# FFN stage of an early-fusion block: rows and gelu turned by transposing DMA transfers, with one step more between an image's parts

## What is computed

```python
def act_quant(x):
    scale = 127.0 / jnp.clip(jnp.max(jnp.abs(x), axis=-1, keepdims=True), 1e-05, None)
    return jnp.clip(jnp.round(x * scale), -128.0, 127.0) / scale
def bitlinear(x, w, g):
    xn = rmsnorm(x, g)            # x * rsqrt(mean(x*x) + 1e-6) * g
    return einsum('bsd,fd->bsf', act_quant(xn), weight_quant(w))
h = h + bitlinear(gelu(bitlinear(layernorm(h), w1, g1)), w2, g2)
```

## Time and profile before

| | us |
|---|---|
| median of 3 runs (lowest, highest) | 1649.14 (1647.32, 1652.2) |
| the profiled execution | 1650.61 |
| its span, first to last instruction | 1648.8 |
| busy over the span: PE, DVE, ACT, POOL | 1470.4, 1337.6, 1301.8, 1113.9 |
| granted TensorE clock, mean | 0.926 |
| FFN stage: from the first `v2` to the end of the span | about 436 |

### The profile page before, as it was taken

How to read it: one execution, slowest core, us unless ns; L and a number is a source line. 1 busy time by engine, 2 the same in 40 slices (tenths; PEclk the granted TensorE clock), 3 DMA queues, 4 the chain that set the end, 5 groups by cost and what they waited for, 6 DMA issues and landing times. The chain is left out here.

```text
span 1648.8 us, 54578 instructions
## 1 busy us (share of the span) xinstructions
PE 1470.4 (89%) x18602; PEld 1180.7 (72%) x18602; DVE 1337.6 (81%) x2848; ACT 1301.8 (79%) x2183; POOL 1113.9 (68%) x1495
## 2 busy tenths in 40 slices
PE   5799999999999999999999999999766777777775
PEld 2678888887887888888888888888655655555554
DVE  5488888888887887887888888887578999999996
ACT  1377877887877878878878878877578999999997
POOL 5456666666666666666666666666367888888886
PEclk8799999999999999999999999999767788878787
DMA  8434334343343343343343343342100000000001
GB/s 215 77 63 68 55 70 65 56 71 63 58 71 61 61 70 60 63 69 58 63 71 56 63 71 56 64 71 40 50 22 26 25 28 28 25 25 25 30 25 31
DMA packets 104195, 93.58 MB, mean 57 GB/s; under 512 B 22737, under 2 KB 94466, under 8 KB 104162
## 3 DMA queue, kind: packets, MB, share of 16 engines
q1 hardware_dynamic: 103394, 91.58, 29.4%
q0 software_dynamic: 768, 1.57, 0.4%
HBM read 74.12 MB, written 11.91 MB: 52 GB/s over the span
## 5 line engine op out<-in xcount | busy, mean ns | idle before, releaser
L1108 PE MATMUL ps<-w_eff,pix 124*112 124x193 f32 (+1 forms) x2048 | 408.4, 338 | 9.8 <-DMA pix<-side 7.3
L713 DVE TENSOR_REDUCE nmax<-ps 116x12 bf16<-116x1344 f32 (+2 forms) x192 | 302.9, 1577 | 117.2 <-PE ps L1203 117.1
L929 ACT ACTIVATE probs<-ps,isw 116x688 f32<-116x688 f32 x384 | 299.1, 832 | 80.5 <-PE ps L1230 79.7
L431 POOL TENSOR_TENSOR xsq<-xsq 124x784 f32<-124x784 f32 (+1 forms) x128 | 184.4, 1440 | 245.3 <-ACT xsq L922 240.3
L518 POOL TENSOR_TENSOR pix<-probs,g_b 112x192 f32<-112x192 f32 (+1 forms) x512 | 309.1, 634 | 40.8 <-ACT probs L1074 30.4
L1108 PEld LDWEIGHTS ps<-w_eff,pix 124*112 124x112 f32 (+1 forms) x2048 | 309.2, 167 | 36.6 <-issue 21.5
L461 POOL TENSOR_SCALAR_AFFINE_SELECT probs<-probs 116x464 f32<-116x464 f32 x384 | 227.8, 610 | 22.3 <-ACT probs L929 19.0
L911 ACT ACTIVATE pix<-xpix 54x896 f32<-54x896 f32 (+1 forms) x128 | 196.9, 1541 | 1.5
L1165 PE MATMUL ps<-xnT,wq_pad 97*128 97x228 f32 (+1 forms) x768 | 166.5, 366 | 0.0
L1334 PE MATMUL ps<-w1t,xpix 96*112 96x384 f16 (+1 forms) x512 | 132.2, 418 | 19.4 <-DVE xpix L809 17.9
L1165 PEld LDWEIGHTS ps<-xnT,wq_pad 97*128 97x128 f32 (+1 forms) x768 | 142.2, 192 | 3.1
(11 more groups left out here) (142 smaller groups left out, 3032.4 us busy)
## 6 DMA issues: line engine op xcount, KB each, us to landing
xpix<-in_x SPq DMA_DIRECT2D x192, 196.0 KB
rden<-den_rows SPq DMA_DIRECT2D x256, 85.5 KB, 2.1
out<-xpix SPq DMA_DIRECT2D x64, 87.0 KB
out<-xpix SPq DMA_DIRECT2D x64, 84.0 KB
xpix<-in_x SPq DMA_DIRECT2D x128, 34.1 KB
h_all<-shift_w SPq DMA_DIRECT2D x5, 768.0 KB, 13.1
pix<-side SPq DMA_DIRECT2D x64, 36.8 KB
pix<-side SPq DMA_DIRECT2D x64, 36.6 KB
```

The source lines that it names most:

```text
L431: nc.gpsimd.tensor_tensor(out_, a, b, ALU.add).then_inc(s_ssq, 1)
L713: V.tensor_reduce(dst, src, AX_X, ALU.max, negate=True).then_inc(s_mx, 1)
L929: A(probs[0:TB, g, 2 * e:2 * e + 2, :], ps[0:TB, 4 + 2 * e:6 + 2 * e, 0:SK], ACT.Exp, scale=isw[0:TB, 7:8]).then_inc(s_p, 1)
L1108: last = MM(ps_tok[tile][0:P, :], pix[0:HI, par, o, lo:lo + P], w_eff[0:HI, o, :], start=(o == 0), stop=(o == OFFS - 1))
```

## The change

- The transposes on PE and both copies out of PSUM (DVE L809, ACT L1067) are gone. SP starts a transposing DMA transfer for each instead, SBUF to SBUF: `q1T` from `q1` (128 rows of 512 float16, 4 blocks of 128 columns) and `q2T` from `q2` (128 rows of 1,536, 12 blocks). `q1`, `q1T`, `q2`, `q2T` have two buffers each. SP's step: store `y` of i-4, turn `q1` of i+1, turn `q2` of i-2.
- The 1536 stays in the turned values. In the first product, a row of `w1t` holds the weights' column sums and meets a column of -1536 in `q1`; the contraction is now split 128 and 65, not 96 and 96. In the second, a product of one row (K = 1) goes ahead of each tile's six. The column sums are made once, ahead of the stage (`weight_columns`: 10 products on PE, two copies on ACT). `w1_t` is laid out for this on the host.
- One step more between an image's parts: in step i, DVE makes `q2`'s scales for i-2 and `y` of i-4; ACT quantises i-2, then does the gelu and the squares of i; PE does the first product of i and the second of i-3; POOL does `v2` of i, then the roots of i (they were ahead of `v2`, those of i-1), with no wait for `f_r1`.
- DVE: `y` now stands behind the maximum of `v1`.
- Once: three memsets on DVE, two on POOL (rows 96 to 127 of `q2`), and the wait of PE's first product for the column sums. SP's turn of the first `q1` stands ahead of the transfers of the last image's attention.

```diff
...
-        q1 = part(xpix, 768, DIM).bitcast(F16).rearrange("p (t d) -> p t d", t=2)
-        q1T = part(xpix, 960, 2 * TB).bitcast(F16).rearrange("p (t c k) -> p t c k", t=2, c=2)
-        q2T = part(xpix, 1192, NCH * TB).bitcast(F16).rearrange("p (t c k) -> p t c k", t=2, c=NCH)
+        q1_all = part(xpix, 384, 512).bitcast(F16)
+        q1 = [part(xpix, 384 + 256 * b, 256).bitcast(F16) for b in range(2)]
+        q1T = [part(xpix, 896 + 256 * b, 256).bitcast(F16).rearrange("p (k r) -> p k r", r=128) for b in range(2)]
+        v1 = part(xpix, 2176, 4 * DIM).rearrange("p (b t d) -> p b t d", b=2, t=2)
+        q2 = [part(probs_f, 4 * WIDE, HIDDEN).bitcast(F16), part(w_eff_f, 0, HIDDEN).bitcast(F16)]
+        q2T = [part(src, at, HIDDEN).bitcast(F16).rearrange("p (k r) -> p k r", r=128)
+               for src, at in ((xpix, 1408), (w_eff_f, HIDDEN))]
+        ones_h = part(tok_f, 0, 64).bitcast(F16)
+        minus = part(tok_f, 64, 64).bitcast(F16)
+        w2_sum = part(tok_f, 128, DIM // 2).bitcast(F16)
...
+            def turn_first(m, p):
+                sp.wait_ge(f_q1, m + 1)
+                apart(sp)
+                sp.dma_start(q1T[p], q1[p], transpose=True).then_inc(f_t1[p], 16)
+
+            def turn_second(j, p):
+                sp.wait_ge(f_q2, j + 1)
+                apart(sp)
+                sp.dma_start(q2T[p], q2[p], transpose=True).then_inc(f_t2[p], 16)
+
+            def store(n):
+                sp.wait_ge(f_y, n + 1)
+                for tile, (lo, hi) in enumerate(((0, TA), (TA, TOK))):
+                    sp.dma_start(out[bass.ds(n, 1), lo:hi, :].rearrange("a t d -> (a t) d"),
+                                 y[0:hi - lo, tile, :]).then_inc(f_out, 16)
+
+            def ffn_step(i, b, new=True, mid=True, last_=True):
+                if last_:
+                    store(i - 4)
+                if new:
+                    turn_first(i + 1, 1 - b)
+                if mid:
+                    turn_second(i - 2, b)
+
             for n in range(IMAGES - 5, IMAGES):
+                if n == IMAGES - 1:
+                    ffn_step(-1, 1, mid=False, last_=False)
                 step_images(n, n % 2, place=n + 4 < IMAGES, load=False)
...
-            with sp.Fori(0, IMAGES) as n:
...
+            ffn_step(0, 0, mid=False, last_=False)
...
+            with sp.Fori(2, PAIRS - 1) as t:
+                for b in range(2):
+                    ffn_step(2 * t + b, b)
...
+            ffn_step(IMAGES + 3, 1, new=False, mid=False)
...
-            def ffn_step(i, b, mid=True):
-
-                if mid:
-                    pool.wait_ge(f_ssq, 2 * i)
-                    nc.gpsimd.tensor_tensor(roots[:, bass.ds(i * 4 + 6, 2)], gel_sum[:, 1 - b, :], expo[:, 0:2],
-                                            ALU.pow).then_inc(f_r1, 1)
...
-            ffn_step(0, 0, mid=False)
+            pool.wait_ge(s_front, IMAGES)
+            pool.wait_ge(s_o, GROUPS * IMAGES)
+            pool.wait_ge(s_rms, IMAGES - 1)
+            for k in range(2):
+                nc.gpsimd.memset(q2[k][96:128, :], 0.0).then_inc(f_rows, 1)
+                pool.wait_ge(f_rows, k + 1)
+
+            def ffn_step(i, b):
+
+                after(pool, f_q2, i - 1)
+                for tile, P in enumerate((TA, TB)):
+                    pool.wait_ge(f_g, 2 * i + tile + 1)
+                    if tile == 1:
+                        pool.wait_ge(f_v2, 2 * i + 1)
+                    for lo in range(0, HIDDEN, HIDDEN // 4):
+                        cols = slice(lo, lo + HIDDEN // 4)
+                        last = nc.gpsimd.tensor_tensor(v2[0:P, b, tile, cols], gel[0:P, b, tile, cols],
+                                                       g2_b[0:P, cols], ALU.mult)
+                    last.then_inc(f_v2, 1)
+                pool.wait_ge(f_v2, 2 * i + 2)
+                pool.wait_ge(f_ssq, 2 * i + 2)
+                nc.gpsimd.tensor_tensor(roots[:, bass.ds(i * 4 + 14, 2)], gel_sum[:, b, :], expo[:, 0:2],
+                                        ALU.pow).then_inc(f_r1, 1)
+
+            ffn_step(0, 0)
             ffn_step(1, 1)
             ffn_step(2, 0)
+            row_roots(IMAGES - 1)
             ffn_step(3, 1)
-            row_roots(IMAGES - 1)
-            with pool.Fori(2, PAIRS - 1) as t:
+            with pool.Fori(2, PAIRS) as t:
                 for b in range(2):
                     ffn_step(2 * t + b, b)
-            ffn_step(IMAGES - 2, 0)
-            ffn_step(IMAGES - 1, 1)
-            ffn_step(IMAGES, 0)
...
+            step(V.memset(ones_h, 1.0))
+            step(V.memset(minus, -MAGIC16))
+            step(V.memset(q1_all, -MAGIC16))
...
-            def copy_rows_turned(m):
...
             def weigh_steps(i, b):
-                after(dve, f_g, 2 * i)
+                after(dve, f_g, min(2 * i, 2 * IMAGES) if isinstance(i, int) else 2 * i)
                 V.tensor_tensor(ff_st[:, b, 40:44], ff_st[:, b, 28:32], w_step[:, :], ALU.mult).then_inc(f_step, 1)
 
-            def ffn_step(i, b, new=True, mid=True, last_=True, turned=True, steps_=True, between=None, skipped=0):
-
-                m, j, st = i + 1, i - 1, ff_st[:, b, :]
+            def ffn_step(i, b, new=True, mid=True, last_=True, steps_=True, between=None, skipped=0):
+
+                m, j, st = i + 1, i - 2, ff_st[:, b, :]
                 flinks[:] = [0, (i + 1) * F_LINKS - skipped]
                 if new:
-                    after(dve, f_q1, m - 1)
                     for tile, P in enumerate((TA, TB)):
                         ins = V.scalar_tensor_tensor(v1[0:P, b, tile, :], h_all[0:P, hcols(m, tile)],
                                                      mean2[0:P, bass.ds(m * 2 + tile, 1)], g1_b[0:P, :],
                                                      ALU.add, ALU.mult)
                     flinks[0] += 1
                     ins.then_inc(f_vc, 1)
+                if steps_:
+                    weigh_steps(i - 1, 1 - b)
+                if between is not None:
+                    between()
+                if new or mid:
+                    after(dve, f_q2, i - 3)
+                if new:
+                    dve.wait_ge(f_vc, flinks[1] + flinks[0])
+                    ins = V.tensor_reduce(st[0:TB, 24:26], v1[0:TB, b, :, :], AX_X, ALU.max,
+                                          apply_absolute_value=True)
                 if last_:
-                    o = i - 3
-                    dve.wait_ge(f_step, o + 3)
+                    o = i - 4
+                    dve.wait_ge(f_step, i)
                     dve.wait_ge(f_m2, o + 1)
                     after(dve, f_out, 32 * o)
...
                     for tile in range(2):
                         dve.wait_ge(f_v2, 2 * j + tile + 1)
-                        ins = V.tensor_reduce(st[0:TB, 26 + tile:27 + tile], v2[0:TB, 1 - b, tile, :], AX_X,
+                        ins = V.tensor_reduce(st[0:TB, 26 + tile:27 + tile], v2[0:TB, b, tile, :], AX_X,
                                               ALU.max, apply_absolute_value=True)
                 if new or mid:
                     flink(ins)
                     if mid:
-                        dve.wait_ge(f_r1, i)
+                        dve.wait_ge(f_r1, j + 1)
                     flink(V.tensor_tensor(st[:, 48:56:2], roots[:, bass.ds(i * 4 + 4, 4)], st[:, 24:28], ALU.mult))
...
-                    after(dve, f_t1, m)
+                    after(dve, f_m1, 2 * m - 2)
                     for tile in range(2):
-                        ins = V.tensor_scalar(q1[0:TB, tile, :], v1[0:TB, b, tile, :], st[0:TB, 36 + tile:37 + tile],
-                                              MAGIC16, ALU.mult, ALU.add)
+                        ins = V.tensor_scalar(q1[1 - b][0:TB, 256 * tile:256 * tile + DIM], v1[0:TB, b, tile, :],
+                                              st[0:TB, 36 + tile:37 + tile], MAGIC16, ALU.mult, ALU.add)
                     ins.then_inc(f_q1, 1)
...
+            def weight_columns():
+                act.wait_ge(f_wsum, 1)
+                A(w1t[REST:REST + 1, 1, :].rearrange("p (c d) -> p c d", c=2), ps[REST:REST + 1, 6:8, 0:HIDDEN // 2],
+                  ACT.Copy).then_inc(f_wcol, 1)
+                act.wait_ge(f_wsum, 2)
+                A(w2_sum[0:1, :], ps[0:1, 0, 0:DIM], ACT.Copy).then_inc(f_wcol, 1)
+
+            def quantise(j, b):
+
+                act.wait_ge(f_sc, j + 4)
+                after(act, f_m2, j - 1)
+                for tile in range(2):
+                    ins = A(q2[b][0:TB, HIDDEN * tile:HIDDEN * (tile + 1)], v2[0:TB, b, tile, :], ACT.Copy,
+                            bias=MAGIC16, scale=ff_st[0:TB, b, 38 + tile:39 + tile])
+                ins.then_inc(f_q2, 1)
+
+            def ffn_step(i, b, new=True, mid=True):
                 if mid:
-                    quantise(i, b, 0)
-                    quantise(i, b, 1)
-                if squares:
+                    quantise(i - 2, b)
+                if new:
+                    after(act, f_v2, 2 * i - 2)
```

(63 more changed lines are left out.)

159 lines of the change are left out of this document (50 added, 109 removed).

## The result

| | before | changed |
|---|---|---|
| median, us | 1648.23 | 1661.32 (1660.98 to 1661.72) |
| ratio, 95% interval | | 1.0072 (1.0058 to 1.0086) |
| profiled execution's span | 1648.8 | 1659.6 |

A forecast was written before the change was run, and what follows sets the result against it. POOL was taken as the bound, its step falling from 6.55 to 6.22 us with waits: 64 x 6.22 + 1.1 - 423.85 + 2.0 + 2.1 = -20.5 from 1650.61, so 1630.1, median forecast 1628 us (chance 0.50), range 1618 to 1672.

The forecast's parts named there:

- L2: Time from the end of ACT's `quantise` to `q2T` in place by transposing DMA; taken as 4.7 us.
- 7.3 + L2: Chain `y`, maxima, scales, `quantise`, transfer, second product, in us over two steps at clock 0.81; 6.0 a step, hidden.
- 8.0 + L2: The same chain from `y` to the next `y` two steps on, in us, with PE at 1.2 GHz.
- rival (a): Transfer latency returns as waits at DVE's `y` and ACT's `quantise`: slower, 1667 us, 1690 at half clock; chance 0.22.
- L2 = 5.8: Transfer time in us at which the step would equal the old pace, P = 6.54; margin 1.1 us.
- PE as no bound: PE, 73% busy, loses 16 transposes an image, gains two one-row products; gain shows only in hand-overs.
- the two bounds: For `q2T`'s transfer: 3.4 us at the stores' rate, 6.3 us at 38 ns per 256-byte piece.
- Rival (c): SP's queue bounds: 16 issues an image, one per 128-column block, 7.7 us a step with stores; 1723 us, chance 0.11.
- POOL is bound at 98%: POOL's own step before the change can't go under 6.44 of 6.55 us; turned round it becomes 6.10.
- Rival (b): POOL's idle gaps stay: longer `v2` pieces and the branch still showing; 6.45 us a step, 1643 us, chance 0.13.
- The extra step: Schedule shift said to give the `quantise` to `y` chain two steps, not one; without it 12 us stand in each.
- The ends: Stage start +2.0 us for column sums and first products; stage end +1.9 for the transfer, +0.2 for one-row products.

## Why the prediction was wrong

**The step that failed** is the sum of the loop for L2: "at the granted clock of 0.81 the mean is 7.3 + L2". Two of its terms were wrong. The clock of before was carried over to a kernel that takes the transposes away from PE; it is 0.50. And the second product was given "plus a sixth for the one-row products", 2.5 us in all at the half clock; it took 3.0, since the two one-row products take 0.40 each and have gaps of their own, 0.85 in place of 0.36. Neither error is enough by itself. At the half clock the prediction's own 8.0 + L2, with the 4.4 measured, is 6.2 a step, no more than the forecast, and the run without the one-row products came to 1633; at the full clock the runs with them came to 1627. Together they make 6.45. The rest to the measured 6.6 is `y`, maxima and scales, 3.8 in place of 3.5, and that the second product starts when the first ends, 0.25 behind the landing.

The prediction named the clock in its rival (a), but priced it only together with a transfer of 6.3 us, and its deciding point, "L2 = 5.8", was wrong: at the half clock the pace of before is reached at an L2 of 5.1 by its own expression, and of 4.6 with the second product's 3.0.

**PE as no bound.** "It isn't the bound before (73% busy), and its gain shows only in hand-overs" is wrong for the kernel after. The first product, held until the gelu has left its banks, stands ahead of the second in PE's order, and with it the circle is closed over PE without the gelu's transfer. The halved transfer shows this: the loop is no shorter.

**The transfer's price** was near: 4.4 against 4.7. At the stage's end, where PE has nothing else to do, it is 3.8, from 1648.68 to 1652.49:

```profile
1646.92 1.76 ACT L1093 ACTIVATE w_eff<-pix,ff_st 116x768 f16<-116x768 f32 x2 [4.40 <-DVE ff_st L898]
...
1652.49 0.40 PE L1382 MATMUL ps<-tok_t 1*112 1x192 f16 x1 [3.13 <-DMA w_eff<-w_eff]
```

The small packets added 42% of 16 x 340 us over 109,771, 21 ns each, between the 14 and the 38 of the two bounds; the 26.9 MB that came with them moved at 189 GB/s where the stores moved 297. The Trainium skill's rule that a transposing transfer is as fast as a plain one (Advanced Engine Details and Errata, X-Bar Transpose (TRN2)) doesn't hold here by a third. Its 1,309 ns for a block (VectorE: DVE Perf Modes, The three transpose paths) is mostly latency, as read: 12 blocks land in 3.7 us and 4 in 2.4, 0.16 us for each further block. Rival (c) is out: a turn is one issue of 1.2 to 1.45 us, with SP idle between.

**DVE and ACT** came out as costed: at the full clock the step is 5.91, DVE's own, forecast at 5.98. **POOL** was put at 6.10 and can do under 5.91. Its gap ahead of the roots fell to 0.20, forecast at 0.36, and turned round alone in the kernel before its step was worth nothing: "POOL is bound at 98%" took three engines that wait for each other for one. Rival (b) is out.

**The extra step** was given a cover that it doesn't provide. In the runs without it no 12 us stand in a step; the chain of `quantise` and `y` spans two steps in either schedule.

**The ends.** The start cost 3.4 us and not 2.0:

```profile
1212.66 2.81 PE L1372 MATMUL ps<-w1t,xpix 128*112 128x384 f16 x8 [2.51 <-ACT tok_t L1086]
1212.78 1.37 POOL L548 MEMSET probs<- 32x1536 f16 x1
...
1214.21 1.38 POOL L548 MEMSET w_eff<- 32x1536 f16 x1
1214.32 0.90 ACT L1105 ACTIVATE probs<-ps,ff_st 112x768 f32<-112x768 f32 x1 [1.70 <-PE ps L1372]
```

The first gelu starts 3.3 us later than in the earlier trace rows and not 2.3, for the most part because the first tile's products took 1.7 to its start, where 0.7 was forecast: the whole product takes 2.8, as at the half clock. POOL's two memsets hold the first `v2` for another 0.4: the gelu's first tile is done at 1215.22, the second memset at 1215.59.

The end cost 5.2 and not 2.1. The landing adds 1.0 (3.8 in place of 2.8) and the slow second product 0.9 there; the rest, 3.3, is DVE's order. The last `v2` is done at 1641.74, but its maxima stand behind the `y` of two images earlier:

```profile
1643.62 0.74 DVE L882 SCALAR_TENSOR_TENSOR xpix<-ps,ff_st,h_all 112x192 f32<-112x192 f32 x2 [2.41 <-PE ps L1384]
1644.28 1.80 DVE L889 TENSOR_REDUCE ff_st<-pix 116x1 f32<-116x768 f32 x2
```

"The extra step of the schedule costs nothing else there" overlooked that; without the step the end is 3.2 us shorter.

That the kernel with added products has the forecast's time, 1627, is no proof of the sum: there the stretch of the `v2` is 31 us shorter than before and the ends 6.8 longer, against 25 and 4 in the forecast, and the clock is one that the forecast didn't have. No run shows the changed kernel at the clock of 0.81 without added work; with dead transposes, or with 12 products and half a turn, at 0.82 and 0.80, it took 1650 and 1652.

## What to carry to other kernels

Work taken from TensorE can cost the clock of what stays on it. Before such a change is priced, put every product that remains in a loop at the half clock, price the small ones by themselves and not by their share of the arithmetic (here 0.40 us for one row against 0.20 for each of the 128-row products behind it), and look for the loop that is then longest, even if the engine is far from full.

If the clock falls, products that nobody reads are a cheap test of whether that is the cause. Here they also give the best version of this study: 1627 to 1628 us, 1.0 to 1.4% under the kernel before, at 12 or 24 a step, while 12 such products in the kernel before cost 0.9%.

An order of waits that "only" shifts work by a step should be followed for each wait by hand: which parts move apart, and which keep their distance.

## What the runs showed of the hardware that was not expected

The clock was steady over the stage: 0.50 in every one of the changed kernel's stretches from 1300 us on, 1.00 in all of those with 24 added products. At a clock in between (0.76 to 0.85) the single executions spread over 19 us (dead transposes) and 10 us (12 products, half a turn), those of the changed kernel over 0.7 and of 24 products over 3.1. With 12 products they lie within 6 us but for one in each of the two runs, at 1642.6 and 1639.2.

It didn't follow the amount of work on PE alone. With the same products in exchanged order it was 0.74 in place of 0.50, and with two products fewer 0.56. With the extra step undone, 12 added products gave 0.81 and not 1.00.

A transposing transfer of half the size went with a loss of the full clock at 12 added products and not at 24. No run here says why.
